# Row maxima in 64-row tiles and bf16, and another order on VectorE, in the output phase of an attention and recurrence kernel

## The chip, the cores and the metric

The kernel runs on one core of a Trainium2 chip. The metric is the device time of one execution in microseconds (us). In the rows PE is TensorE (matmul), PEld its weight loads, DVE is VectorE, ACT is ScalarE, POOL is GpSimd and SP is SyncE, which here issues the DMA transfers. L2267 is line 2267 of the kernel before.

## The reference

The input is x of 16 images, 64 by 64 positions, 128 channels. A first layer normalises x in channel groups, runs a two-dimensional recurrence over rows and columns and adds its result to x. The second layer takes the 4096 positions of an image as tokens t:

```
t = t + attention(ln(t))
t = t + ffn(ln(t))

attention: q, k, v = heads(ln(x) @ w_qkv), 8 heads of 16
           q_l, k_l = means of q and k over 64 landmarks
           attn1 = softmax(q @ k_l.T)        # 4096 x 64 for each head
           out = attn1 @ pinv(softmax(q_l @ k_l.T)) @ (softmax(q_l @ k.T) @ v)
           out = (out + conv33(v)) @ w_out + b_out
           return x + out
ffn:       Wx = x @ W.T, normalised with the statistics of all tokens,
           y_t = sigmoid(Wx_t + y_(t-1) @ V.T) along the tokens
```

The change touches attn1, the product with it, and the addition of the convolution.

## The kernel before

The program has phases one after the other: group norm, the recurrence over rows and columns, landmarks, pseudo-inverse (which also sets up constants for the next phase, class `Early`), output, and the final recurrence. The change lies in the output phase, and for one small constant at the end of the pseudo-inverse phase.

The output phase goes through the 16 images in 8 chunks of 512 tokens (NG = 8, GT = 4 tiles of 128 tokens). Every engine has its own program, a loop of 128 slots written out by hand; in each slot an engine works at several chunks at once, at different stages (`slot(b, c, ...)` handles chunk c + 1 for the row maxima, c for the scores and exponentials, c - 1 for reciprocals and merge, c - 2 for normalise and the addition of the convolution, c - 3 for the projection, c - 4 and c - 5 for the ffn). Engines run their instructions in order and meet only through semaphores; `wait(eng, name, count)` waits until `name` was raised count times. `nth(b, c)` is the running number of a chunk, from 1.

The stages of a chunk, with the engine and the line in the profile:

- GpSimd copies the queries to bf16, o_q_lp (L1931). kb_lp holds the keys of the landmarks in bf16 with the channels of other heads zeroed: 128 channels by 8 heads by 64 landmarks.
- TensorE, `row_maxima` (L2008): for each of the 4 token tiles one matmul of 128 channels, 128 tokens and 512 columns (8 heads of 64 landmarks), into the banks bank_l[0] and bank_l[1] in turn. Pairs of tiles are issued at two places in the slot.
- VectorE, `maxima` (L2230): a maximum over the 64 landmarks of each head, into o_m1 (in the rows o_m), 128 tokens by 128 places, of which two in each 16 are used.
- TensorE, `turn_maxima` (L2014): four transposes of o_m1 into bank_l[0]; ScalarE, `negate` (L2145), copies them with the opposite sign to o_negm in bf16.
- TensorE, `scores`: a matmul with o_negm (L2025) and then one with the queries (L2029) into the four banks bank_s; ScalarE takes exponentials (L2188) into o_p.
- TensorE, `weigh` (L2039): eight tiles of 64 rows and 32 columns side by side give the weighed values and the denominators; ScalarE copies them to `even` and `odd` (L2166, L2168).
- GpSimd masks `even` into o_pvs (L1937). SyncE packs the denominators by DMA, VectorE takes their reciprocals (L2273), SyncE spreads them to memory and broadcasts them back as o_rden.
- VectorE, `merge` (L2278): att = odd x keep + pvs. `normalise` (L2284): att = att x rden.
- The convolution of v: TensorE `convolve` (L2051), ScalarE `copy_convolved` (L2150) into o_res, TensorE `turn_convolved` (L2060) into bank_y. VectorE `add_convolved` (L2267): oT = att + bank_y.
- TensorE `project` (L2067) into bank_x; VectorE `residual` (L2243, then bn_stats and bn_aggr, L2249, into o_mv); GpSimd `norm`: o_vare (L1944), o_z (L1946), o_r (L1949), o_z again (L1951).
- TensorE `turn_normed` (L2074), ScalarE L2173, TensorE `ffn` (L2080), which writes bank_y and so waits until add_convolved has read it; ScalarE `copy_wx` (L2182); VectorE `statistics` (L2254, once per image also L2259).

TensorE's order in a slot is: scores, row maxima (two tiles), ffn, project, row maxima (two tiles), weigh, queries (L1999), turn_maxima, convolve, turn_convolved, turn_normed. VectorE's order is: four maxima, residual, reciprocals, merge, normalise, statistics, add_convolved. Once per image GpSimd also sets the next image's kb_lp (L1911), pairs and contexts (slots 2 to 5).

The functions that the diff touches:

Of the kernel before, what the change touches and what calls it, by code (L numbers as in the profile page):

```python
# [6 lines left out]
BF16 = mybir.dt.bfloat16  # L7
# [4 lines left out]
P = 128  # L12
# [1326 lines left out]
class Early:  # L1339


    def __init__(self, m, sems):
        self.w = m.sb("o_wq", [C, C])
        self.wo = m.sb("o_wo", [C, C])
        self.fw = m.sb("o_fw", [C, C])
        self.bout = m.sb("o_bout", [P, C])
        self.bands = m.sb("o_bands", [P, HEADS, LM])
        self.v = [[m.sb(f"o_v{k}{f}", [P, NT // 2, VROW]) for f in range(2)] for k in range(2)]
        self.xnT = [m.sb(f"o_xnT{k}", [C, 512]) for k in range(4)]
        self.bs = [m.sb(f"o_base{k}", [P, GT, C]) for k in range(4)]  # L1350
        self.pair_mask = m.sb("o_pair_mask", [C, 2, LM])
        self.kb_lp = [m.sb(f"o_kb_lp{k}", [C, HEADS, LM], BF16) for k in range(2)]
        self.zb = [m.sb(f"o_zb{k}", [P, PAIRS_H, 2 * DH]) for k in range(2)]
        self.keep = [m.sb(f"o_keep{h}", [P, 1]) for h in range(2)]
        self.ind = m.sb("o_ind", [P, 2, LM], BF16)
        self.m1 = m.sb("o_m1", [P, GT, P])
        self.half = m.sb("o_half", [P, GT])
        self.eps = m.sb("o_eps", [P, GT])
        self.one = m.sb("o_one", [P, 1])
        self.s = {n: sems.sem("o_" + n) for n in ("w", "const", "mask", "pair", "keep", "setup")}  # L1360
        self.s_band = sems.sem("o_band")
        self.s_v = [sems.sem(f"o_v{k}") for k in range(2)]
        self.s_xl = [sems.sem(f"o_xl{k}") for k in range(4)]
        self.s_bl = [sems.sem(f"o_bl{k}") for k in range(4)]
# [15 lines left out]
def pinv_phase(nc, sems, R, E, band, xnt, tokens, vals, taps, wqkv, w_out, b_out, ffn_wT):  # L1380
# [7 lines left out]
    with ExitStack() as ctx:  # L1388
# [267 lines left out]
        def _(dve):  # L1656
# [36 lines left out]
            for k in range(PINV_ITERS):  # L1693
# [7 lines left out]
                for c in LATE:  # L1701
                    if k + 1 < PINV_ITERS:
                        first_product(nc.vector, k + 1, c - 2, 0, s_ta)
                    last_product(k, c)
            nc.vector.tensor_reduce(E.pair_mask[:, :, :], R.head_mask[:, :, :].rearrange("c (g a) l -> c a l g", a=2), AX.X, ALU.add
                                    ).then_inc(E.s["pair"], 1)
            for h in range(2):
                taken = R.ident[:, DH * (1 - h):P:QUAD]
                nc.vector.tensor_reduce(E.keep[h][:, :], taken, AX.X, ALU.add).then_inc(E.s["keep"], 1)
                dve.wait_ge(E.s["keep"], 2 * h + 1)  # L1710
                nc.vector.tensor_scalar(E.keep[h][:, :], E.keep[h][:, :], -1.0, 1.0, ALU.mult, ALU.add).then_inc(E.s["keep"], 1)
# [6 lines left out]
def output_phase(nc, sems, R, E, xnt, tokens, vals, recips, t2, wx, wx_stats):  # L1718


    with ExitStack() as ctx:
# [268 lines left out]
        def _(pe):  # L1990
            pe.wait_ge(s["w"], 64)
            pe.wait_ge(s["const"], CONST)
            pe.wait_ge(s["mask"], PAIRS_H)

            def queries(b, c):

# [1 line left out]
                wait(pe, "qc", nth(b, c) - 1)  # L1998
                nc.tensor.matmul(bank_q[:, :], w[:, :], xnT[c % 4][:, :], start=True, stop=True).then_inc(s["qm"], 1)  # L1999

            def row_maxima(b, c, k, q):

                if k == 0:
                    wait(pe, "ql", nth(b, c))
                    wait(pe, "setup", SETUP * (b + (c == NG) + 1))
                    wait(pe, "neg", nth(b, c) - 1)
                wait(pe, "max", GT * (nth(b, c) - 1) + k - 1)
                nc.tensor.matmul(bank_l[k % 2][:, :], q_lp[c % 2][:, P * k:P * k + P],  # L2008
                                 kb_lp[q][:, :, :].rearrange("c h l -> c (h l)"), start=True, stop=True).then_inc(s["lp"], 1)

            def turn_maxima(b, c):
                wait(pe, "max", GT * nth(b, c))
                for k in range(GT):
                    mt = nc.tensor.transpose(bank_l[0][:, P * k:P * k + P], m1[:, k, :], R.ident[:, :])  # L2014
                mt.then_inc(s["mt"], 1)

            def scores(b, c, q):
# [64 lines left out]
            def slot(b, c, q, first, last):  # L2082
                scores(b, c, q)
                nq = q if c + 1 < NG else 1 - q
                if follows(c, 1, last):
                    row_maxima(b, c + 1, 0, nq)
                    row_maxima(b, c + 1, 1, nq)
                if precedes(c, 5, first):
                    ffn(b, c - 5)
                if precedes(c, 3, first):  # L2090
                    project(b, c - 3)
                if follows(c, 1, last):
                    row_maxima(b, c + 1, 2, nq)
                    row_maxima(b, c + 1, 3, nq)
                weigh(b, c, q)
                if follows(c, 3, last):
                    queries(b, c + 3)
# [11 lines left out]
            for c in range(NG):  # L2109
                wait(pe, "convc", c - 2)  # L2110
                convolve(0, c, bank_s[c % 3][:, :])
                if c in (1, 3):
                    queries(0, (c + 1) // 2)
                if c >= GT:
                    row_maxima(0, 0, c - GT, 0)
            turn_maxima(0, 0)
            wait(pe, "convc", NG)
            each_image(pe, slot)
# [103 lines left out]
        def _(dve):  # L2222
# [1 line left out]

            dve.wait_ge(s["keep"], 4)

            def maxima(b, c, k):
                wait(dve, "lp", GT * (nth(b, c) - 1) + k + 1)
                wait(dve, "mt", nth(b, c) - 1)
                nc.vector.tensor_reduce(m1[:, k, :].rearrange("p (g r) -> p g r", r=QUAD)[:, :, 0:2],  # L2230
                                        bank_l[k % 2][:, :].rearrange("p (g a l) -> p g a l", g=PAIRS_H, a=2), AX.X, ALU.max
                                        ).then_inc(s["max"], 1)

            def residual(b, c):
# [51 lines left out]
            def slot(b, c, q, first, last):  # L2286
# [4 lines left out]
                    residual(b, c - 3)  # L2291
                if precedes(c, 1, first):
                    reciprocals(b, c - 1)
                    merge(b, c - 1)
                if precedes(c, 2, first):
                    normalise(b, c - 2)
                if precedes(c, 5, first):
                    if c == 5 and b:
                        wait(dve, "stats", b)
                    statistics(b, c - 5)  # L2300
                if precedes(c, 2, first):
                    add_convolved(b, c - 2)
            for k in range(GT):
                maxima(0, 0, k)
            each_image(dve, slot)
# [310 lines left out]
```

## Time and profile before

| | |
|---|---|
| median of 3 runs | 6138.11 us (6130.87 to 6140.42) |
| profiled execution | 6141.54 us, span 6139.9 us |
| busy share of the span | PE 88%, ACT 52%, DVE 48%, POOL 30% |
| mean granted TensorE clock | 0.973 |
| output phase | first to last L2025 start, 2676.8 to 3776.0 us |

Busy shares of the whole span are means over phases with different limits; the final recurrence alone, after about 3830 us, leaves VectorE and GpSimd nearly idle. The rows further down are therefore taken from the output phase. A timeline row gives the start in us, the duration in us, engine, line, operation and operands, the count of instructions merged into the row, and in brackets the idle time of the engine before it and what ended it. The durations of TensorE's rows include a latency that overlaps the next group, so distances between starts are the better measure there.

### The profile page before, as it was taken

To read this page: it belongs to the slowest core of one execution; us is meant where nothing else is said; L and a number is where in the kernel's file an instruction comes from. 1 tells how busy PE (TensorE), PEld (TensorE's weight loads), DVE (VectorE), ACT (ScalarE), POOL (GpSimd) and SP (SyncE) were. 2 spreads that over 40 slices of the span, in tenths; PEclk is the share of its full clock that TensorE was granted. 3 is DMA by queue.
4 is the path that set the end of the run, shared out by engine and by line. 5 is a ranking of instruction groups with operands and counts; after the bars stand their busy time and mean duration, and the time that the engine had idled before them with its cause. 6 is when DMAs were issued, how large, how long until landed. Compare 5 with 4: busy or idle time off the path is not lost. (4 is left out here: it accounts for less than half of the span.)

```text
span 6139.9 us, 218886 instructions
## 1 busy us (share of the span) xinstructions
PE 5411.7 (88%) x89728; PEld 3294.7 (54%) x89728; DVE 2953.7 (48%) x7658; ACT 3195.0 (52%) x9222; POOL 1817.5 (30%) x2146
## 2 busy tenths in 40 slices
PE   5599999997899998789999997888888888888888
PEld 4499888996566665654555443333333333333333
DVE  8577666774777775458888886000000000000000
ACT  5455555564666665358888885333333333333333
POOL 2000000002877774248888886000000000000000
PEclk7799999998999999999999998999999999999999
DMA  8731111225777773347777775011111211111111
GB/s 352 282 108 60 56 56 63 76 84 179 238 232 230 217 230 103 94 127 219 220 219 223 217 219 151 26 44 46 44 46 44 60 45 46 44 46 44 46 46 44
DMA packets 857415, 756.44 MB, mean 123 GB/s; under 512 B 71024, under 2 KB 732528, under 8 KB 853360
## 3 DMA queue, kind: packets, MB, share of 16 engines
q1 hardware_dynamic: 840784, 640.78, 35.0%
q0 software_dynamic: 14208, 101.45, 4.1%
q8 instruction: 711, 11.65, 0.8%
q14 instruction: 272, 2.23, 0.1%
q10 hardware_dynamic: 1440, 0.33, 0.0%
HBM read 425.72 MB, written 308.45 MB: 120 GB/s over the span
## 5 line engine op out<-in xcount | busy, mean ns | idle before, releaser
L2554 ACT ACTIVATE f_y<-f_acc 128x16 f32<-128x16 f32 x4096 | 753.7, 184 | 1548.1 <-PE f_acc L2523 1548.1
L2523 PEld LDWEIGHTS f_acc<-f_y,f_vT 128*32 128x32 f32 x32768 | 647.0, 108 | 1493.0 <-ACT f_y L2554 1482.2
L2523 PE MATMUL f_acc<-f_y,f_vT 128*32 128x16 f32 x32768 | 1048.1, 193 | 297.9 <-issue 9.5
L2512 PE MATMUL f_junk<-f_idle 128*32 128x512 bf16 x12368 | 1228.4, 377 | 2.0 <-issue 1.9
L2470 DVE TENSOR_TENSOR f_sum<-f_turned,f_t 128x512 f32<-128x512 f32 x128 | 88.6, 692 | 1758.6 <-PE f_turned L2505 1758.5
L2230 DVE TENSOR_REDUCE o_m<-o_bank_l 128x8 f32<-128x512 f32 x512 | 329.4, 685 | 183.7 <-PE o_bank_l L2008 182.3
L533 POOL DMA_DIRECT2D hidden<-l_h x48 | 36.2, 756 | 1200.0 <-DVE l_hsum L733 973.3
L2512 PEld LDWEIGHTS f_junk<-f_idle 128*32 128x32 bf16 x12368 | 368.9, 99 | 2.2 <-issue 2.2
L1170 ACT ACTIVATE a_p<-a_s 128x512 f32<-128x512 f32 x512 | 264.2, 602 | 149.6 <-PE a_s L1055 149.6
L656 ACT ACTIVATE l_gate<-l_pf,l_bf 128x256 f32<-128x256 f32 (+7 forms) x512 | 202.3, 446 | 240.2 <-PE l_pf L583 215.8
L2188 ACT ACTIVATE o_p<-o_bank_s 128x512 f32<-128x512 f32 x512 | 264.4, 602 | 84.8 <-PE o_bank_s L2029 84.8
L2460 DVE TENSOR_SCALAR f_wxn<-f_wx,f_scale,f_shift 128x2048 f32<-128x2048 f32 x32 | 83.9, 2623 | 383.4 <-DMA f_wx<-wx 343.7
L573 PE MATMUL l_pf<-l_x,l_wf 128*128 128x256 f32 (+7 forms) x1024 | 240.2, 357 | 6.6 <-ACT l_gate L656 6.6
L1230 DVE TENSOR_REDUCE a_m3p<-a_s 128x1 f32<-128x512 f32 x384 | 235.6, 676 | 17.9 <-PE a_s L1031 17.9
L2505 PE MATMUL f_turned<-f_ident,f_y 128*32 128x128 f32 x4096 | 224.4, 292 | 1.0 <-issue 0.8
L2494 PE MATMUL f_acc<-f_wxn,f_ident 128*32 128x128 f32 x4096 | 210.2, 278 | 13.0 <-DVE f_wxn L2460 13.0
L941 POOL TENSOR_TENSOR a_r<-a_vare,a_half 128x8 f32<-128x8 f32 x128 | 209.6, 1638 | 10.0
L2158 ACT ACTIVATE o_base<-o_base,r_loss,r_gain 128x128 f32<-128x128 f32 x512 | 211.9, 506 | 0.0
L573 PEld LDWEIGHTS l_pf<-l_x,l_wf 128*128 128x128 f32 x1024 | 185.0, 191 | 23.6 <-ACT l_gate L656 7.8
L659 ACT ACTIVATE l_tanhc<-l_cell 128x256 f32<-128x256 f32 (+7 forms) x256 | 101.0, 395 | 177.8 <-DVE l_cell L709 177.8
L1946 POOL TENSOR_TENSOR o_z<-o_t,o_mv 128x512 f32<-128x512 f32 x128 | 186.4, 1457 | 0.0
L2080 PE MATMUL o_bank_y<-o_zT,o_fw 128*128 128x512 f32 x256 | 138.3, 622 | 35.9 <-DVE o_oT L2267 34.5
(280 smaller groups left out, 11906.8 us busy)
## 6 DMA issues: line engine op xcount, KB each, us to landing
o_v<-vals SPq DMA_DIRECT2D x256, 272.0 KB, 3.4
a_hid<-hidden SPq DMA_DIRECT2D x112, 520.0 KB, 4.7
hidden<-l_h POOLq DMA_DIRECT2D x48, 1040.0 KB, 6.2
skew<-gn_skew POOLq DMA_DIRECT2D x8, 6144.0 KB, 23.2
l_x<-skew SPq DMA_DIRECT2D x46, 1024.0 KB, 5.2
vals<-a_v SPq DMA_DIRECT2D x128, 272.0 KB, 3.5
gn_x<-in_x SPq DMA_DIRECT2D x16, 2048.0 KB, 15.5
a_xin<-in_x SPq DMA_DIRECT2D x128, 256.0 KB, 4.5
```

The lines of the kernel that those rows point to most:

```text
L573: mm = nc.tensor.matmul(banks[c][g][:, :, rows], w[W[g]][:, :], xs, start=g in (0, 2, 3), stop=False, skip_group_check=True)
L941: pool.tensor_tensor(r[:, :, :], vare[:, :, :], half[:, :, :], ALU.pow).then_inc(s["pow"], 1)
L1170: nc.scalar.activation(p3[c % 2][g][:, :], S[g][:, :], ACT.Exp).then_inc(s["exp"], 1)
L1230: nc.vector.tensor_reduce(m3p[:, g, c:c + 1], bank[:, :], AX.X, ALU.max).then_inc(s["mx"], 1)
L2158: nc.scalar.activation(bs[c % 4][:, k, :], bs[c % 4][:, k, :], ACT.Identity, scale=R.gain[:, b, n:n + 1], bias=R.loss[:, b, n:n + 1]).then ...
L2188: nc.scalar.activation(p1[g][:, :], bank_s[g][:, :], ACT.Exp).then_inc(s["exp"], 1)
L2230: nc.vector.tensor_reduce(m1[:, k, :].rearrange("p (g r) -> p g r", r=QUAD)[:, :, 0:2], bank_l[k % 2][:, :].rearrange("p (g a l) -> p g a ...
L2494: mm = nc.tensor.matmul(acc[k % 2][rows, PT * piece:PT * piece + PT, :], ident[:, rows], wxn[q][:, at, :], start=piece == 0, stop=False, s ...
L2505: mt = nc.tensor.matmul(turned[g % 2][rows, b % 4, :], y[q][:, rows, b], ident[:, :], start=True, stop=True)
L2512: nc.tensor.matmul(junk[rows, :], idle[:, 0:QUAD], idle[:, :], start=True, stop=True)
L2523: mm = nc.tensor.matmul(acc[k % 2][rows, t, :], vT[:, rows], before, start=False, stop=True, skip_group_check=True)
L2554: nc.scalar.activation(y[q][:, u, :], acc[u // RC % 2][:, u % RC, :], ACT.Sigmoid).then_inc(s_y, 1)
```

## The change

Row maxima: each token tile's matmul is split in two by channels, 64 rows with the four heads that have their channels there. The lower half of the channels writes bank_l[0], the upper half bank_l[1], and each bank now holds four heads of two token tiles. VectorE's maxima run over such a bank. o_m1 is bf16, and is turned by a matmul with a bf16 identity in place of an f32 transpose; the identity is cast once at the end of the phase before. On VectorE normalise and add_convolved come before merge and statistics.

```diff
-        self.m1 = m.sb("o_m1", [P, GT, P])
+        self.m1 = m.sb("o_m1", [P, GT, P], BF16)
+        self.ident_lp = m.sb("o_ident_lp", [P, P], BF16)
...
+            nc.vector.tensor_copy(E.ident_lp[:, :], R.ident[:, :]).then_inc(E.s["pair"], 1)
...
+            pe.wait_ge(s["pair"], 2)
...
-            def row_maxima(b, c, k, q):
+            def row_maxima(b, c, r, q):
-                if k == 0:
+                if r == 0:
                     wait(pe, "ql", nth(b, c))
                     wait(pe, "setup", SETUP * (b + (c == NG) + 1))
                     wait(pe, "neg", nth(b, c) - 1)
-                wait(pe, "max", GT * (nth(b, c) - 1) + k - 1)
-                nc.tensor.matmul(bank_l[k % 2][:, :], q_lp[c % 2][:, P * k:P * k + P],
-                                 kb_lp[q][:, :, :].rearrange("c h l -> c (h l)"), start=True, stop=True).then_inc(s["lp"], 1)
+                for k in range(2):
+                    for half in range(2):
+                        if k == 0:
+                            wait(pe, "max", GT * (nth(b, c) - 1) + 2 * r + half - 1)
+                        rows, heads = slice(LM * half, LM * half + LM), slice(PAIRS_H * half, PAIRS_H * half + PAIRS_H)
+                        token = P * (2 * r + k)
+                        ml = nc.tensor.matmul(bank_l[half][:, 2 * P * k:2 * P * k + 2 * P], q_lp[c % 2][rows, token:token + P],
+                                              kb_lp[q][rows, heads, :].rearrange("c h l -> c (h l)"), start=True, stop=True)
+                        if k == 1:
+                            ml.then_inc(s["lp"], 1)
...
-                    mt = nc.tensor.transpose(bank_l[0][:, P * k:P * k + P], m1[:, k, :], R.ident[:, :])
+                    mt = nc.tensor.matmul(bank_l[0][:, P * k:P * k + P], m1[:, k, :], E.ident_lp[:, :], start=True, stop=True)
...
                 if follows(c, 1, last):
                     row_maxima(b, c + 1, 0, nq)
-                    row_maxima(b, c + 1, 1, nq)
...
                 if follows(c, 1, last):
-                    row_maxima(b, c + 1, 2, nq)
-                    row_maxima(b, c + 1, 3, nq)
+                    row_maxima(b, c + 1, 1, nq)
...
-            def maxima(b, c, k):
-                wait(dve, "lp", GT * (nth(b, c) - 1) + k + 1)
+            def maxima(b, c, n):
+                r, half = n // 2, n % 2
+                wait(dve, "lp", GT * (nth(b, c) - 1) + n + 1)
                 wait(dve, "mt", nth(b, c) - 1)
-                nc.vector.tensor_reduce(m1[:, k, :].rearrange("p (g r) -> p g r", r=QUAD)[:, :, 0:2],
-                                        bank_l[k % 2][:, :].rearrange("p (g a l) -> p g a l", g=PAIRS_H, a=2), AX.X, ALU.max
+                nc.vector.tensor_reduce(m1[:, 2 * r:2 * r + 2, LM * half:LM * half + LM].rearrange("p k (g r) -> p k g r", r=QUAD)[:, :, :, 0:2],
+                                        bank_l[half][:, :].rearrange("p (k g a l) -> p k g a l", k=2, g=2, a=2), AX.X, ALU.max
...
                     reciprocals(b, c - 1)
-                    merge(b, c - 1)
                 if precedes(c, 2, first):
                     normalise(b, c - 2)
+                    add_convolved(b, c - 2)
+                if precedes(c, 1, first):
+                    merge(b, c - 1)
                 if precedes(c, 5, first):
                     if c == 5 and b:
                         wait(dve, "stats", b)
                     statistics(b, c - 5)
-                if precedes(c, 2, first):
-                    add_convolved(b, c - 2)
```

Ahead of the first image the row maxima are issued in two groups in place of four.

## Rows read from the trace of the kernel before

**Rows 1.** The tile o_negm: count, duration ns min/median/max, first and last start us.
```profile
L2025 PE MATMUL o_bank_s<-o_negm,o_ind x512: 371/384/385, 2676.8 to 3776.0; 32*128 32x512 bf16 x171
```

**Rows 2.** Busy us of each engine in one stretch, granted clock, DMA share, GB/s.
```profile
3000.00:3100.00 100.00, 99.17 (x755) 50.77 (x740) 83.68 (x215) 83.65 (x175) 89.71 (x88) 1.00 0.77 222
```

**Rows 3.** Timeline of TensorE, one slot.
```profile
3021.09 0.39 PE L2025 MATMUL o_bank_s<-o_negm,o_ind 32*128 32x512 bf16 x4
3021.32 1.02 PE L2029 MATMUL o_bank_s<-o_qT,o_kb 32*128 32x512 f32 x8
3022.28 0.61 PE L2008 MATMUL o_bank_l<-o_kb_lp,o_q_lp 128*128 128x512 bf16 x2
3022.72 1.02 PE L2080 MATMUL o_bank_y<-o_zT,o_fw 128*128 128x512 f32 x2
3023.58 1.05 PE L2067 MATMUL o_bank_x<-o_wo,o_oT 128*128 128x128 f32 x8
3024.47 0.59 PE L2008 MATMUL o_bank_l<-o_kb_lp,o_q_lp 128*128 128x512 bf16 x2
3024.99 1.09 PE L2039 MATMUL o_bank_s<-o_p,o_zb 64*32 64x512 f32 x16
3026.01 1.12 PE L1999 MATMUL o_bank_s<-o_xnT,o_wq 128*128 128x512 f32 x2
3026.97 0.60 PE L2014 MATMUL o_bank_l<-r_ident,o_m 128*128 128x128 f32 x4
3027.50 1.11 PE L2051 MATMUL o_bank_s<-o_v,o_bands 128*64 128x256 f32 x8
3028.54 0.66 PE L2060 MATMUL o_bank_y<-r_ident,o_res 128*128 128x128 f32 x4
...
3029.57 0.39 PE L2025 MATMUL o_bank_s<-o_negm,o_ind 32*128 32x512 bf16 x4
```

**Rows 4.** Timeline of VectorE, the same slot.
```profile
3022.70 1.29 DVE L2230 TENSOR_REDUCE o_m<-o_bank_l 128x8 f32<-128x512 f32 x2 [0.47 <-PE o_bank_l L2008]
3024.88 1.29 DVE L2230 TENSOR_REDUCE o_m<-o_bank_l 128x8 f32<-128x512 f32 x2 [0.89 <-PE o_bank_l L2008]
...
3028.28 0.66 DVE L2278 SCALAR_TENSOR_TENSOR o_att<-o_odd,o_keep,o_pvs 128x512 f32<-128x512 f32 x1
3028.85 0.69 DVE L2284 TENSOR_TENSOR o_att<-o_att,o_rden 128x512 f32<-128x512 f32 x1
...
3030.06 0.67 DVE L2267 TENSOR_TENSOR o_oT<-o_att,o_bank_y 128x512 f32<-128x512 f32 x1
```

**Rows 5.** Timeline of ScalarE, the same slot.
```profile
3022.42 2.06 ACT L2188 ACTIVATE o_p<-o_bank_s 128x512 f32<-128x512 f32 x4 [0.63 <-PE o_bank_s L2029]
...
3028.66 0.60 ACT L2150 ACTIVATE o_res<-o_bank_s 128x512 f32<-128x512 f32 x1 [0.22 <-PE o_bank_s L2051]
```

**Rows 6.** Timeline of GpSimd, the same slot.
```profile
3028.21 0.79 POOL L1944 TENSOR_TENSOR o_vare<-o_mv,o_eps 128x4 f32<-128x4 f32 x1 [0.94 <-DVE o_mv L2249]
3028.95 1.49 POOL L1946 TENSOR_TENSOR o_z<-o_t,o_mv 128x512 f32<-128x512 f32 x1
3030.40 1.01 POOL L1949 TENSOR_TENSOR o_r<-o_vare,o_half 128x4 f32<-128x4 f32 x1
```

**Rows 7.** Timeline of all engines, the slot after kb_lp is set.
```profile
3050.69 1.28 POOL L1911 TENSOR_TENSOR o_kb_lp<-r_head_mask,r_k_lm 128x512 bf16<-128x512 f32 x1
...
3054.13 0.75 DVE L2278 SCALAR_TENSOR_TENSOR o_att<-o_odd,o_keep,o_pvs 128x512 f32<-128x512 f32 x1 [0.32 <-POOL o_pvs L1937]
3054.20 1.58 POOL L1946 TENSOR_TENSOR o_z<-o_t,o_mv 128x512 f32<-128x512 f32 x1
3054.80 1.53 DVE L2284 TENSOR_TENSOR o_att<-o_att,o_rden 128x512 f32<-128x512 f32 x1
3055.75 1.46 POOL L1949 TENSOR_TENSOR o_r<-o_vare,o_half 128x4 f32<-128x4 f32 x1
...
3057.67 1.10 PE L2080 MATMUL o_bank_y<-o_zT,o_fw 128*128 128x512 f32 x2 [0.83 <-DVE o_oT L2267]
```

More of the change, by code:

```diff
@@ L2113, in _ @@
                     queries(0, (c + 1) // 2)
-                if c >= GT:
-                    row_maxima(0, 0, c - GT, 0)
+                if c in (GT, GT + 2):
+                    row_maxima(0, 0, (c - GT) // 2, 0)
             turn_maxima(0, 0)
```

## The prediction

> **What bounds the kernel now.** I first looked up where the touched lines run. Everything in the diff, apart from one small cast, lies in the output phase: the first and last start of the bank_s matmuls fed by o_negm [rows 1] are 1099.2 us apart for 128 chunks, so 127 slots (a slot is the work of one 512-token chunk) take 8.655 us each. The share table of one stretch in the middle [rows 2] shows TensorE busy 99% at a granted clock of 1.00, GpSimd 90%, VectorE and ScalarE 84% each, and the DMA engines 77%. So TensorE comes first, but nobody is idle by more than a sixth: whatever TensorE gives up, another engine may take back.
>
> TensorE's timeline of one slot [rows 3] has no wait in it. From bank_s at 3021.09 to the next at 3029.57 is 8.48 us. I read it by distances between starts, since the rows' own durations include a latency that overlaps the next group. The first pair of row-maxima matmuls takes 0.44 (3022.28 to 3022.72), the second 0.52, the turn of the maxima 0.53. Two 512-column bf16 matmuls in 0.44 make 0.21 each, and eight 128-column f32 passes (L2067) in 0.89 make 0.11 each.
>
> VectorE in the same slot [rows 4] waits twice for row-maxima matmuls, 0.47 and 0.89 us, so it needs 8.48 - 1.36 = 7.1. ScalarE [rows 5] starts its exponentials at 3022.42 and ends the copy of the convolution, which the next scores need, at 3029.26. GpSimd [rows 6] waits 0.94 for VectorE's bn_aggr before o_vare.
>
> One slot per image is different [rows 7]. GpSimd first makes the next image's kb_lp (1.28 us), is late for o_pvs, VectorE's merge starts late, its normalise takes 1.53 us instead of 0.69, add_convolved is late, and the ffn matmul on TensorE, which overwrites the bank that add_convolved reads, waits 0.83. The mean slot of 8.655 against the regular 8.48 is this: 8 x 0.175 = 1.4 us per image, 22 us in 16 images.
>
> **The change, part by part, per slot.**
>
> *Row maxima in 64-row tiles.* Four matmuls of 128 rows by 512 columns become eight of 64 rows by 256 columns, in four pairs whose members use different rows and different banks. No 64-row bf16 pair is in the trace. The nearest row is L2029: eight f32 passes over 512 columns on four row groups take 0.96 us (3021.32 to 3022.28), where two such passes on all rows (L2080) take 0.86 [rows 3]. Four row groups thus run side by side, and so should two. Then four pairs of 256 columns stream 4 x 0.107 = 0.43 in place of 0.85: a saving of 0.43. Bounds: 0 if pairs do not overlap, 0.43 if they do.
>
> *Changes of tile shape.* Where the shape of the tile stays, groups follow each other at the streaming time: L2008 to L2080 0.44 for 0.43 streamed, L2080 to L2067 0.86. Where it changes, about 0.1 is added: L2029 (32 rows) to L2008 (128) 0.96 instead of 0.86, L2008 to L2039 (64 by 32) 0.52 instead of 0.43, L2039 to L1999 1.02 instead of 0.86 [rows 3]. The new row maxima put a 64 by 128 shape ahead of the ffn matmul and after project, where there was no change before. Two more changes at 0.1 cost 0.2. Bounds 0 and 0.3 (two of L2039's 0.16). I take 0.2. The Trainium skill (TensorEngine Tiling, Key Properties) says that changing the tiling mode drains TensorE, which speaks against this part of the change; it has no price, the rows agree with it, and without it the sum would be 0.2 per slot lower.
>
> *The turn in bf16.* Four f32 passes in 0.53, of which about 0.1 is the change to the 128 by 64 shape behind it. bf16 halves the streaming: the bf16 matmul took 0.21 for 512 columns, so four of 128 stream 0.21 instead of 0.43. Weight loads may keep it from showing; L1999 to L2014 has another 0.1 that may go with the transposing form. Bounds 0 and 0.3; I take 0.2.
>
> TensorE's slot without waits is then 8.48 - 0.43 + 0.2 - 0.2 = 8.05 (bounds 7.75 and 8.58).
>
> *ScalarE.* From the first exponential to the end of the convolution's copy 6.84, of which 0.22 is a wait; then bank_s, scores and the next exponential, 1.33 after the matmul starts [rows 3, 5]: 6.62 + 0.06 + 1.33 = 8.01, a little under 8.05. No charge.
>
> *VectorE, the maxima.* The same 512 elements from one bank and eight results; writing bf16 costs and saves nothing that I can see in a reduce bound by its input. 0. The first result comes after the third of four small matmuls, about when the first big one ended: 0.
>
> *VectorE, the order.* After the reciprocal came merge, normalise, statistics, add; now normalise, add, merge, statistics. The work is the same, so the gain is only that add is earlier by a merge and a statistics (0.6 + 0.6). That removes the 0.83 wait of the ffn matmul [rows 7]. What comes with it: add now directly follows normalise, whose result it needs, a start distance of about 0.72 instead of 0.60; and add needs the turned convolution (L2060), which ends at 3029.20; the instruction after the reciprocal starts at 3028.28 [rows 3, 4]. Measured from the second pair of row maxima (3024.47) that end is 4.73, less 0.2 and 0.1 of the savings behind it 4.43; add is ready 3.81 + 0.72 = 4.53 after it. Hidden, by 0.1.
>
> *VectorE against GpSimd.* In regular slots o_vare and o_z are stretched while merge and normalise run: z takes 1.49 [rows 6], and ends 0.9 after normalise does. In the late slot z took 1.58, and then normalise took 1.53: it had to wait for z, ending 0.55 after z did; add and the maxima, with one operand in PSUM, are never stretched [rows 4, 7]. So the two engines exclude each other when VectorE reads two operands from SBUF. The Trainium skill (SBUF — State Buffer, Who interferes with whom) states just this, that whoever starts first holds the port for its whole instruction; these rows agree. In the new order (n is the start of normalise) o_vare is blocked until n + 0.68, z starts at n + 0.7 and nothing blocks it during add, so it runs to n + 1.74. Merge is ready at n + 1.3 and is blocked until then: it ends at n + 2.3 instead of n + 1.85, 0.45 later. Bounds 0 and 0.85 (the stretched normalise). I take 0.45.
>
> Does VectorE still fit? Its loop is: the second row maxima start on TensorE, 0.41 until the reduce starts (3024.47 to 3024.88), 5.18 to add's start, 0.6 to its end, then two more maxima, 1.29, and 0.06 until TensorE may overwrite the second bank [rows 3, 4]. That is 7.54, plus 0.45 blocked = 7.99. Under 8.05, by very little.
>
> *GpSimd.* z gets 0.45 shorter (1.49 to 1.04), r 0.45 longer as it now runs into the blocked merge (1.01 and 1.46 in [rows 6, 7]). Zero in sum. Its wait of 0.94 shrinks by the slot's 0.43 to 0.51.
>
> *Once per image.* kb_lp takes GpSimd 1.28 [rows 7], with the step to the next instruction about 1.35; 0.51 is cover, so about 0.85 reaches normalise (now the first to meet a late GpSimd), less 0.06 of VectorE's slack: 0.8. wx_stats is written by one more VectorE instruction, about 0.2. Together 1.0 per image instead of 1.4, 0.12 per slot.
>
> *Other parts.* The cast of the identity in the phase before, and a wait for it, fall where VectorE has nothing else due: under 0.3 us once. No DMA is moved; SyncE's spread still follows the reciprocal, which keeps its place, and the DMA share rises to 0.77 x 8.48 / 8.17 = 0.80.
>
> **The sum.** Regular slot 8.05, mean 8.17. 127 x (8.655 - 8.17) = 62 us. The profiled execution took 6141.5 us (span 6139.9), so 6080; the median of the runs, 6138.1, lies 3.4 below it, so 6077.
>
> **The rivals.**
> - *The pairs do not overlap* (or weight loads, twice as many, fill the time). TensorE 8.48 + 0.2 - 0.2 = 8.48; only the ffn wait goes, say 17 us: 6121. Against it: L2029.
> - *Nothing takes back the gain*: no price on tile changes, merge not blocked or absorbed. 7.85, mean 7.96, 88 us: 6050. For it: VectorE's 7.54 would allow it. Against: 0.1 shows at each shape change, and ScalarE's 8.01 would have to give.
> - *Slower*: GpSimd stays late in every slot, so that normalise waits for the rest of o_pvs as well as merge for z. At the 0.85 of the late slot VectorE's loop is 7.99 + 0.85 = 8.84, 127 x 0.185 = 24 us more: 6162. It decides once GpSimd's cover of 0.51 is gone in regular slots and normalise loses over 0.67 in each. Against it: a longer slot gives GpSimd its cover back, so the state should heal itself.
> - *VectorE sets the pace*, with TensorE near 7.9: mean 8.15, 6075, the same number by another road.
>
> **Chances and range.** My forecast (TensorE or VectorE at 8.0 to 8.15, so 6062 to 6095) 0.52; pairs or tile changes eating most of the gain (6095 to 6125) 0.20; the whole gain (6040 to 6062) 0.15; no change 0.04; slower 0.09. A measurement of this kernel tells about 0.2% (12 us) from no change. The range 6045 to 6115 leaves out the slower case, no change, and the ends of the two beside. Faster by over 0.2%: 0.87; within: 0.04; slower: 0.09.
>
> **What would show it.** Starts of the row-maxima groups: first to ffn about 0.33, second to weigh about 0.33, with project to row maxima 0.95. The turn to the convolution about 0.33. No wait of the ffn matmul for o_oT. Merge (L2278's line) near 1.1 us, o_r near 1.46, o_z near 1.04. VectorE's wait ahead of the first maxima nearly gone. I am wrong if the four small matmuls of a group take 0.43 or more, or if normalise is stretched in regular slots, or if TensorE waits for o_m in every slot.

## The result, and the profile after

The changed kernel takes 6087.5 us (median of 4 runs, 6082.1 to 6091.8) against 6138.7 for the kernel before: ratio 0.9918, 95% interval 0.9904 to 0.9932, so 0.8% or 51 us faster. The forecast was 6077 in a range of 6045 to 6115.

The gain lies in the output phase. The tile o_negm in the trace of the changed kernel (count, duration ns min/median/max, first and last start us):

```profile
L2035 PE MATMUL o_bank_s<-o_negm,o_ind x512: 371/384/385, 2674.2 to 3726.8; 32*128 32x512 bf16 x171
```

1052.6 us for 127 slots, 8.288 each, where [rows 1] gave 8.655: 46.6 of the 51.3 us between the two profiled executions (6141.5 and 6090.2). The other 4.7 us lie before the first slot and after the last. The share table of the stretch of [rows 2] (us, PE, PEld, DVE, ACT, POOL, clock, DMA share, GB/s):

```profile
3000.00:3100.00 100.00, 98.64 (x822) 49.67 (x816) 88.11 (x218) 85.97 (x181) 90.58 (x90) 1.00 0.80 229
```

TensorE is still full, VectorE went from 84 to 88%, the DMA engines from 77 to 80%. One regular slot on TensorE, beside [rows 3]:

```profile
3003.76 0.39 PE L2035 MATMUL o_bank_s<-o_negm,o_ind 32*128 32x512 bf16 x4
3003.99 1.02 PE L2039 MATMUL o_bank_s<-o_qT,o_kb 32*128 32x512 f32 x8
3004.95 0.39 PE L2016 MATMUL o_bank_l<-o_kb_lp,o_q_lp 64*128 64x256 bf16 x4
3005.27 1.12 PE L2090 MATMUL o_bank_y<-o_zT,o_fw 128*128 128x512 f32 x2
3006.23 1.05 PE L2077 MATMUL o_bank_x<-o_wo,o_oT 128*128 128x128 f32 x8
3007.22 0.39 PE L2016 MATMUL o_bank_l<-o_kb_lp,o_q_lp 64*128 64x256 bf16 x4
3007.54 1.09 PE L2049 MATMUL o_bank_s<-o_p,o_zb 64*32 64x512 f32 x16
3008.56 1.12 PE L2002 MATMUL o_bank_s<-o_xnT,o_wq 128*128 128x512 f32 x2
3009.52 0.39 PE L2024 MATMUL o_bank_l<-o_ident_lp,o_m 128*128 128x128 bf16 x4
3009.84 1.11 PE L2061 MATMUL o_bank_s<-o_v,o_bands 128*64 128x256 f32 x8
...
3011.90 0.40 PE L2035 MATMUL o_bank_s<-o_negm,o_ind 32*128 32x512 bf16 x4
```

The slot is 8.14 instead of 8.48. Group by group, from one group's start to the next one's: first row maxima to ffn 0.32 (was 0.44), second to weigh 0.32 (0.52), the turn 0.32 (0.53). Those are savings of 0.12, 0.20 and 0.21. But two distances grew: ffn to project 0.96 (0.86) and project to row maxima 0.99 (0.89).

VectorE and GpSimd around the same place, beside [rows 4] and [rows 6]:

```profile
3011.05 0.63 DVE L2293 TENSOR_TENSOR o_att<-o_att,o_rden 128x512 f32<-128x512 f32 x1
3011.71 0.69 DVE L2276 TENSOR_TENSOR o_oT<-o_att,o_bank_y 128x512 f32<-128x512 f32 x1
3012.31 0.96 DVE L2287 SCALAR_TENSOR_TENSOR o_att<-o_odd,o_keep,o_pvs 128x512 f32<-128x512 f32 x1
3013.19 0.68 DVE L2263 BATCH_NORM_STATS2 o_fst<-o_wx 128x6 f32<-128x512 f32 x1
3013.80 1.26 DVE L2239 TENSOR_REDUCE o_m<-o_bank_l 128x8 bf16<-128x512 f32 x2
```

```profile
3010.97 0.75 POOL L1946 TENSOR_TENSOR o_vare<-o_mv,o_eps 128x4 f32<-128x4 f32 x1 [0.75 <-DVE o_mv L2258]
3011.69 1.03 POOL L1948 TENSOR_TENSOR o_z<-o_t,o_mv 128x512 f32<-128x512 f32 x1
3012.69 1.46 POOL L1951 TENSOR_TENSOR o_r<-o_vare,o_half 128x4 f32<-128x4 f32 x1
```

Merge runs 0.96 instead of 0.65, until 0.55 after the end of o_z; o_z is 1.03, o_r 1.46; the wait ahead of the first maxima is gone. That is the picture that the prediction drew for a regular slot. What it did not draw is in the table of waits from 2750 to 3700 us (us in total, times, longest):

```profile
PEld o_bank_l L2016 <- DVE o_m L2239: 14.8, 43, 0.5
DVE o_rec_packed L2282 <- DMA o_den_packed<-o_odd: 13.5, 28, 1.2
PE o_bank_l L2016 <- DVE o_m L2239: 5.9, 30, 0.3
PE o_bank_y L2090 <- DVE o_oT L2276: 1.6, 4, 0.8
```

The same table of the kernel before has these lines for the ffn matmul and the reciprocal:

```profile
PE o_bank_y L2080 <- DVE o_oT L2267: 18.5, 27, 0.9
DVE o_rec_packed L2273 <- DMA o_den_packed<-o_odd: 1.6, 4, 0.6
```

The ffn matmul hardly waits any more, but the reciprocal now waits for the packed denominators in 28 slots instead of 4. Distances between slot starts on TensorE split into three kinds: 8.14 to 8.17 in most, 8.4 to 8.6 in most slots after kb_lp, and 27 slots of 8.6 to 9.4. The kernel before had 8.47 to 8.51 in most, one of about 9.55 in 13 of the images (mostly with one of 8.6 behind it), and fourteen more of 9.1 to 9.6.

How a late transfer makes such a slot is seen where the slot that starts at 2869.88 takes 8.70. VectorE, GpSimd and TensorE around it:

```profile
2869.09 0.35 DVE L2282 RECIPROCAL o_rec_packed<-o_den_packed 128x32 f32<-128x32 f32 x1 [0.24 <-DMA o_den_packed<-o_odd]
2869.36 1.32 DVE L2293 TENSOR_TENSOR o_att<-o_att,o_rden 128x512 f32<-128x512 f32 x1
...
2872.58 1.27 DVE L2239 TENSOR_REDUCE o_m<-o_bank_l 128x8 bf16<-128x512 f32 x2
```

```profile
2868.93 0.20 POOL L1946 TENSOR_TENSOR o_vare<-o_mv,o_eps 128x4 f32<-128x4 f32 x1 [0.63 <-DVE o_mv L2258]
2869.08 1.04 POOL L1948 TENSOR_TENSOR o_z<-o_t,o_mv 128x512 f32<-128x512 f32 x1
```

```profile
2873.91 0.39 PE L2016 MATMUL o_bank_l<-o_kb_lp,o_q_lp 64*128 64x256 bf16 x3 [0.17 <-DVE o_m L2239]
```

The reciprocal waits only 0.24, but that makes normalise start 0.28 after o_z instead of ahead of it. Normalise then ends 0.56 after o_z does and takes 1.32 instead of 0.63; the maxima are late, TensorE waits for them in the second group of row maxima, and the slot is 0.56 longer than a regular one. All 27 late slots have such a start: in 21 of them the normalise around the slot's start took over 0.9 (in 14 of these 21 the reciprocal ahead of it had waited for the denominators), and in the other 6 that wait alone was 0.67 or more.

### The profile page after: what moved, and what is told of

Read it like the earlier page. It is cut to its first block and busy times, and to the rows that moved or that the text cites. A ratio compares the mean times of both kernels' runs of the same rounds, so it can differ in the third digit from the quotient of the medians.

```text
span 6088.6 us, 219912 instructions
## 1 busy us (share of the span) xinstructions
PE 5375.2 (88%) x90240; PEld 3269.6 (54%) x90240; DVE 2974.9 (49%) x7659; ACT 3178.0 (52%) x9222; POOL 1809.8 (30%) x2146
## 5 line engine op out<-in xcount | busy, mean ns | idle before, releaser
L2239 DVE TENSOR_REDUCE o_m<-o_bank_l 128x8 bf16<-128x512 f32 x512 | 327.2, 680 | 100.0 <-PE o_bank_l L2016 100.0
L1951 POOL TENSOR_TENSOR o_r<-o_vare,o_half 128x4 f32<-128x4 f32 x128 | 185.7, 1451 | 0.0
L2077 PEld LDWEIGHTS o_bank_x<-o_wo,o_oT 128*128 128x128 f32 x1024 | 136.8, 195 | 61.8 <-issue 61.8
```

Source lines behind the costliest of these rows:

```text
L2239: nc.vector.tensor_reduce(m1[:, 2 * r:2 * r + 2, LM * half:LM * half + LM].rearrange("p k (g r) -> p k g r", r=QUAD)[:, :, :, 0:2], bank_l ...
```

## The experiments

Every ratio is to the kernel before on the same chip. The changed kernel has 0.9918.

**The changed kernel with VectorE's old order.**

```diff
                     reciprocals(b, c - 1)
+                    merge(b, c - 1)
                 if precedes(c, 2, first):
                     normalise(b, c - 2)
-                    add_convolved(b, c - 2)
-                if precedes(c, 1, first):
-                    merge(b, c - 1)
...
                     statistics(b, c - 5)
+                if precedes(c, 2, first):
+                    add_convolved(b, c - 2)
```

> The changed kernel with VectorE's old order (merge, normalise, statistics, add). Theory: TensorE's regular slot stays 8.14 us in streaming, but the addition of the convolution now ends 0.1 to 0.2 us after the ffn matmul could start, so regular slots come to 8.2 to 8.3 and the slot after kb_lp loses over 1 us again; mean slot 8.40, 14 us slower than the changed kernel (about 6102). Rival, that the order brought nothing and TensorE's shorter work everything: within 5 us of the changed kernel (6087). Rival, that the order brought most: 6120 or more.

Measured: 0.9998 (0.9989 to 1.0007). The gain is gone, all of it. Of the times expected only the last, 6120 or more, came true, though the theory's regular slot of 8.2 to 8.3 was nearly met. Its waits and slots say why. TensorE (waits from 2750 to 3700 us):

```profile
PE o_bank_y L2090 <- DVE o_oT L2276: 49.1, 71, 2.8
```

Regular slots are 8.30 to 8.37, not 8.14, since the addition ends too late for the ffn matmul; the slots after kb_lp are about 9.8 in nine images; some twenty others take 9.2 to 9.4, and one 12.6. Two neighbouring slots of it, a regular one and a late one, VectorE, GpSimd and TensorE:

```profile
2740.11 0.65 DVE L2287 SCALAR_TENSOR_TENSOR o_att<-o_odd,o_keep,o_pvs 128x512 f32<-128x512 f32 x1
...
2748.60 1.51 DVE L2287 SCALAR_TENSOR_TENSOR o_att<-o_odd,o_keep,o_pvs 128x512 f32<-128x512 f32 x1
```

```profile
2740.03 0.79 POOL L1946 TENSOR_TENSOR o_vare<-o_mv,o_eps 128x4 f32<-128x4 f32 x1 [0.79 <-DVE o_mv L2258]
2740.78 1.49 POOL L1948 TENSOR_TENSOR o_z<-o_t,o_mv 128x512 f32<-128x512 f32 x1
...
2748.37 0.20 POOL L1946 TENSOR_TENSOR o_vare<-o_mv,o_eps 128x4 f32<-128x4 f32 x1 [0.78 <-DVE o_mv L2258]
2748.52 1.04 POOL L1948 TENSOR_TENSOR o_z<-o_t,o_mv 128x512 f32<-128x512 f32 x1
```

```profile
2752.05 1.10 PE L2090 MATMUL o_bank_y<-o_zT,o_fw 128*128 128x512 f32 x2 [1.17 <-DVE o_oT L2276]
```

In the first slot merge starts 0.08 after o_vare and both of GpSimd's instructions stretch. In the second merge starts 0.23 after it; o_vare and o_z are served first, merge takes 1.51, and the ffn matmul waits 1.17. A tenth or two on VectorE decides which engine pays, and in the old order the addition stands behind both of VectorE's two-operand instructions and passes all of it to TensorE.

**The new order alone, in the kernel before.** The last part of the diff and nothing else.

> The kernel before with only VectorE's new order. Theory: TensorE's 8.48 us per slot stays and binds, only the waits of the ffn matmul go: mean slot 8.52 instead of 8.655, 17 us faster than before (6121). Rival, that the blocked merge costs VectorE as much as the earlier addition gains: 6138 or slower. Merge about 1.0 us instead of 0.65 and o_z 1.04 instead of 1.49 in regular slots under both.

Measured: 0.9950 (0.9936 to 0.9963), 31 us. The direction is right, the size nearly twice what I gave it. o_z is 1.04 in most slots as expected, but merge is 0.7 to 0.8 and not 1.0. Slots are 8.47 to 8.54, and one of about 8.7 per image; both the 9.55 and the fourteen others are gone.

**The turn in bf16 alone, in the kernel before.**

```diff
-        self.m1 = m.sb("o_m1", [P, GT, P])
+        self.m1 = m.sb("o_m1", [P, GT, P], BF16)
...
-                    mt = nc.tensor.transpose(bank_l[0][:, P * k:P * k + P], m1[:, k, :], R.ident[:, :])
+                    mt = nc.tensor.matmul(bank_l[0][:, P * k:P * k + P], m1[:, k, :], E.ident_lp[:, :], start=True, stop=True)
```

> The kernel before with only o_m1 in bf16 and its turn by a bf16 matmul. Theory: the turn takes 0.32 instead of 0.53 between starts, nothing else on TensorE moves: regular slot 8.27 us, once-per-image loss as before or 0.3 more, mean 8.45 to 8.49, 21 to 26 us faster (6112 to 6117). Rival, that a matmul with the identity costs as much as the transpose and the gain in the changed kernel came from the tiles: 6138.

Measured: 0.9984 (0.9975 to 0.9993), 10 us, and so neither the 21 to 26 of the theory nor the nothing of the rival. Regular slots came down to 8.26 to 8.29 as expected, 27 us over 127 slots, but late slots (about 9.75 after kb_lp, others 9.1 to 9.3) took two thirds of it back.

**The changed kernel without 64-row tiles.**

```diff
-                for k in range(2):
-                    for half in range(2):
...
+                nc.tensor.matmul(bank_l[k % 2][:, :], q_lp[c % 2][:, P * k:P * k + P],
+                                 kb_lp[q][:, :, :].rearrange("c h l -> c (h l)"), start=True, stop=True).then_inc(s["lp"], 1)
```

> The changed kernel with the row maxima in 128-row tiles again (bf16 turn and new order stay). Theory: the tiles gave 0.12 us per regular slot and no more (they save 0.12 and 0.20 at their own groups and cost 0.10 each on ffn's and project's way to the next group), so the regular slot is 8.27 and the kernel 12 to 15 us slower than the changed one (about 6100). Rival, that the four pairs saved their full 0.43 and another engine took 0.3 back: TensorE's regular slot above 8.4 and 6110 or more. Rival, that VectorE or the DMAs set the pace anyway: the same 6087.

Measured: 0.9930 (0.9916 to 0.9943), 43 us faster than before and so about 8 slower than the changed kernel; the two intervals overlap. The slot decides between the theories: 8.26 to 8.29 where the changed kernel has 8.14 to 8.17. In this kernel ffn to project is 0.86 again:

```profile
3007.39 1.02 PE L2083 MATMUL o_bank_y<-o_zT,o_fw 128*128 128x512 f32 x2
3008.25 1.05 PE L2070 MATMUL o_bank_x<-o_wo,o_oT 128*128 128x128 f32 x8
3009.14 0.59 PE L2011 MATMUL o_bank_l<-o_kb_lp,o_q_lp 128*128 128x512 bf16 x2
```

So the tiles are worth 0.12 us per slot: they save 0.12 and 0.20 at their own groups and add 0.10 on each side of project. No other engine took 0.3 back.

**Only the second group in 64-row tiles.** The first group is one matmul of 128 rows by 512 columns for each token tile again, and its maxima likewise.

```diff
+                if r == 0:
+                    for k in range(2):
...
+                        nc.tensor.matmul(bank_l[k][:, :], q_lp[c % 2][:, token:token + P],
+                                         kb_lp[q][:, :, :].rearrange("c h l -> c (h l)"), start=True, stop=True).then_inc(s["lp"], 1)
+                    return
```

> The changed kernel with 64-row tiles only for the second group of row maxima (between project and weigh); the first group, between the scores and the ffn matmul, is 128 rows by 512 columns again. Theory from the distances between starts: the first group saves 0.12 at its own place and costs 0.10 on the ffn matmul's way to the next group, so undoing it costs 0.02 us per slot: slots of 8.16, the same time as the changed kernel within 4 us (-0.75 to -0.82%). Rival, that each group of tiles is worth the same: slots of 8.20, 8 us slower than the changed kernel (-0.69%).

Measured: 0.9934 (0.9920 to 0.9948). The slots are 8.15 to 8.19, about 0.02 above the changed kernel's, as the distances said: nearly all that the tiles bring is brought by the second group. The total can't tell the two expectations apart.

**Statistics ahead of merge.**

```diff
                     add_convolved(b, c - 2)
-                if precedes(c, 1, first):
-                    merge(b, c - 1)
...
                     statistics(b, c - 5)
+                if precedes(c, 1, first):
+                    merge(b, c - 1)
```

> The changed kernel with VectorE's order normalise, add, statistics, merge. Merge then starts when o_z on GpSimd is over, so it is not blocked (0.65 instead of 0.89 mean), and VectorE's loop is about 0.4 us shorter. Theory, that in regular slots TensorE sets the pace and the rest comes from late packed denominators: regular slots stay 8.14, the late ones shrink a little because VectorE catches up sooner; 0 to 0.1% faster than the changed kernel (-0.82 to -0.92% against before). Rival, that the blocked merge is what makes late slots: 0.2% or more faster than the changed one.

Measured: 0.9958 (0.9944 to 0.9971), slower than the changed kernel by 0.4%; both expectations failed. Most slots are still 8.14 to 8.16, but thirty take 9.2 or more. In one of them normalise ran 1.32 and merge 1.30, each behind an instruction of GpSimd, and TensorE waited for maxima:

```profile
3017.31 1.32 DVE L2293 TENSOR_TENSOR o_att<-o_att,o_rden 128x512 f32<-128x512 f32 x1
...
3019.88 1.30 DVE L2287 SCALAR_TENSOR_TENSOR o_att<-o_odd,o_keep,o_pvs 128x512 f32<-128x512 f32 x1
...
3021.10 1.27 DVE L2239 TENSOR_REDUCE o_m<-o_bank_l 128x8 bf16<-128x512 f32 x2
```

```profile
3019.59 1.04 POOL L1953 TENSOR_TENSOR o_z<-o_z,o_r 128x512 f32<-128x512 f32 x1
3020.59 1.72 POOL L1961 TENSOR_TENSOR o_base<-o_base,o_bout 128x512 f32<-128x512 f32 x1
```

Merge started 0.3 after GpSimd's second o_z and had to wait for its end. In a regular slot merge is now free, 0.65, as expected. But once normalise has been late, merge meets a second instruction of GpSimd: the late slot costs 1.1 instead of 0.6, and there are thirty of them. In the changed kernel a regular merge meets only the last 0.4 us of the first o_z, which costs no time.

**Packing the denominators early,** in the changed kernel and, as a control, in the kernel before.

```diff
                     spread(b, c - 1)
+                pack(b, c)
...
                     broadcast(b, c - 1)
-                pack(b, c)
```

> The changed kernel with one move on SyncE: the packing of the denominators is issued right behind the spread of the reciprocals, ahead of the loads of v and of the broadcast. Theory, that the slots of 8.7 us and more in the changed kernel come from a reciprocal that waits for the packed denominators (28 waits): these waits vanish, slots stay at 8.14 but for the ones after kb_lp, the mean falls from 8.29 to about 8.18, and the kernel is 0.20 to 0.25% faster than the changed one (-1.05% against before). Rival, that the late slots come from the lock between VectorE and GpSimd: the waits vanish and the time stays at -0.82%. Rival, that the DMA queues are full: the broadcast or the loads of v come late instead, and the time stays or grows.

> The kernel before with the packing of the denominators issued early, as the only edit. Theory: at 8.48 us per slot the denominators are late in 4 slots of 128, so the edit is worth nothing before the change: within 0.1% of before. Rival, that SyncE's order cost something all along: 0.2% or more faster than before.

Measured: 1.0061 (1.0047 to 1.0074) in the changed kernel, 1.0051 (1.0037 to 1.0064) in the kernel before. The third way given for the changed kernel came true; for the control neither expectation did. Waits for packed denominators are gone, and normalise waits for the broadcast instead, first in the changed kernel and then in the kernel before:

```profile
DVE o_att L2293 <- DMA o_rden<-recips: 90.6, 96, 2.4
DVE o_att L2284 <- DMA o_rden<-recips: 26.8, 41, 2.5
```

Lateness moved from one transfer to the other and grew.

**A lighter load of v,** in the changed kernel and in the kernel before.

```diff
+            lanes = slice(0, 1 if light and side else P)
-            sp.dma_start(self.v[half][side][:, GT * piece:GT * piece + GT, :],
-                         vals[b, row:row + 512, :].rearrange("(n p) c -> p n c", p=P)).then_inc(self.s_v[half], 16)
+            sp.dma_start(self.v[half][side][lanes, GT * piece:GT * piece + GT, :],
+                         vals[b, row:row + 512, :].rearrange("(n p) c -> p n c", p=P)[lanes]).then_inc(self.s_v[half], 16)
```

> The changed kernel with a lighter load of v: in the output phase one of the two shifted copies of v is loaded for one partition only (the convolution of the later images is then computed from old data for that copy; every instruction of the engines stays, and so does the number of transfers). Theory, that the changed kernel's slots of 8.7 us and more come from transfers that land late because the DMA engines are at 80%: the waits for the packed denominators go from 28 to under 5, the mean slot falls from 8.29 to about 8.18, 13 to 16 us faster than the changed kernel (about -1.05% against before). Rival, that they come from the lock between VectorE and GpSimd: -0.82% as the changed kernel, within 0.05%.

> The control of the run with the lighter load of v: the same edit in the kernel before (same part of the convolution computed from old data). Theory, that at 8.48 us per slot transfers are in time and the late slots are those of the lock: within 0.15% of before, with slots of 9.2 and 9.55 us still there. Rival, that the DMA engines cost the kernel before just as much: 0.25% or more faster than before.

Measured: 0.9920 (0.9907 to 0.9933) and 0.9998 (0.9989 to 1.0007). The share table of the first, from 2750 to 3700 us:

```profile
2750.00:3700.00 950.00, 941.14 (x7763) 472.36 (x7762) 850.31 (x2073) 820.91 (x1717) 875.96 (x858) 1.00 0.69 195
```

and its wait for the denominators:

```profile
DVE o_rec_packed L2283 <- DMA o_den_packed<-o_odd: 11.8, 22, 1.6
```

The DMA engines went from 80 to 69% busy, and the denominators are late almost as often, 22 times instead of 28. The slots stay as well: 24 of 8.6 and more, against 27. My theory that the load of the DMA engines makes them late fails at this step of load, and the time is that of the rival. In the kernel before the theory was right: no effect on the median that can be measured, and late slots still there. In the profiled execution 5 of the 14 others remain; whether that is the edit or chance is open, as only one execution was traced.

**The loads of v behind the packing.**

```diff
                     spread(b, c - 1)
+                    broadcast(b, c - 1)
+                pack(b, c)
...
-                if precedes(c, 1, first):
-                    broadcast(b, c - 1)
-                pack(b, c)
```

> The changed kernel with SyncE's loads of v behind the broadcast and the packing, so that the small transfers of the reciprocals no longer share the DMA engines with them. Theory, that late small transfers are what makes slots late: the wait of the broadcast for the spread shrinks from 0.8 us, packed denominators land earlier, the mean slot falls by 0.05 to 0.1, 6 to 12 us faster than the changed kernel (-0.95%). Rival, as in the run that packed early, that the loads of v now pile up on the broadcast and make it late: slower than the changed kernel by 10 us or more.

Measured: 1.0276 (1.0258 to 1.0293). Slower, though not by the rival's road: the convolution on TensorE waits for v in every fourth slot, which takes 15 to 18 us. The denominators are not earlier either; the reciprocal waits for them 42 times, 63.3 us.

```profile
PE o_bank_s L2060 <- DMA o_v<-vals: 135.5, 24, 7.0
```

```profile
2750.00:3700.00 950.00, 806.05 (x6258) 406.39 (x6260) 684.29 (x1669) 662.05 (x1383) 692.24 (x694) 0.92 0.63 187
```

**GpSimd relieved.**

```diff
-                pool.tensor_tensor(tile, tile, bout[:, :].unsqueeze(1).broadcast_to([P, GT, C]), ALU.add).then_inc(s["based"], 1)
+                pool.tensor_tensor(tile[:, 0:1, :], tile[:, 0:1, :], bout[:, :].unsqueeze(1), ALU.add).then_inc(s["based"], 1)
```

> The changed kernel with GpSimd's addition of the output bias done for one token tile of four (three quarters of the tokens lack the bias), which frees GpSimd by about 0.9 us in each slot. Theory, that a late GpSimd costs the changed kernel 0.3 us in the slot after kb_lp and little else: 4 to 6 us faster than the changed kernel (-0.9% against before), and slots of 8.7 us still there. Rival, the sum of the prediction, in which kb_lp costs 0.8 us per image: 12 us or more faster (-1.02%).

Measured: 0.9932 (0.9920 to 0.9943), not faster than the changed kernel, so that both expected times were missed. The slots after kb_lp came down to 8.14 in seven of the images, where the changed kernel has that in three; that is the 0.3 us that the theory gave them, but there are 40 slots of 8.6 and more instead of 27, with 33 waits for denominators, 20.4 us. Why a freer GpSimd brings more of these waits was not looked into. The prediction's 0.8 us per image for a late GpSimd does not show, here or in the slots of the changed kernel.

## Why the prediction was right, and where its sum was off

The forecast of 62 us met 51, and the sign, the engine that sets the pace and the shape of a regular slot were right. Yet its terms were wrong by more than the sum shows, and that they met is partly luck. In the sum TensorE's shorter slot (8.48 to 8.05) made 55 us and the order 7. Measured one after the other, the order made 31, the turn on top of it about 12 and the tiles about 8. (The sum's upper bound for TensorE's slot should also have been 8.78, not 8.58: 8.48 + 0.3 with nothing saved.)

- **Row maxima in tiles: too large.** The pairs do overlap: a group takes 0.32, as forecast. The step that failed is "Two more changes at 0.1 cost 0.2". I had one cost at the end of the first group, inside its 0.33, and one behind project. Both came, and a third with them, 0.10 between ffn and project, where the shape does not change. Net 0.12 us per slot instead of 0.23 (the untiled run: 8.27 against 8.14), 15 us of streaming in place of 29. [rows 3] had a row for it. L1999, which also follows narrow tiles, takes 0.96 to the next group instead of 0.86, and I had put that down to the transposing turn behind it. In the traces it is the first matmul behind the change that is longer: 0.53 to the next matmul's start, in L1999 of both kernels and in the ffn of the changed one, against 0.43 in the ffn of regular slots before and in the untiled run. The Trainium skill (TensorEngine Tiling (Array Packing), Key Properties) says that changing the tiling mode drains TensorE. The costs here agree with it, as those on both sides of project are gone without the tiles; it gives no price.
- **The turn: right for the regular slot,** 0.21 against 0.20, which is 27 us over 127 slots. Under the new order only about 12 of them reached the time, and 10 under the old one; late slots took the rest. The other 0.1, from L1999 to the turn, stayed with the transposing form gone: 0.96 in both kernels.
- **The new order: too small.** The sum gave it 7 us (1.0 us per image instead of 1.4), a rival the 0.83 wait in one slot per image, 17 us; alone it gave 31. The step that failed is "The mean slot of 8.655 against the regular 8.48 is this", which reads one kind of late slot only. That mean hides that the last image's slots are shorter, and that fourteen more slots were late. In 7 of these fourteen merge took over 1.2, in 5 others normalise: they lost the race against o_z. I had shown the lock in both directions but only priced it in the new order.
- **The parts are not a sum.** With the old order, 0.33 less in TensorE's slot brings nothing (0.9998). Order alone 31 us, tiles and turn alone 1 us, together 51. The order is what lets TensorE's saving through. In [rows 3, 4] the addition ends at 3030.73 and the next ffn matmul is due at 3022.72 + 8.48 = 3031.20, so it was 0.47 ahead; the savings that lie between the second row maxima and the ffn matmul are 0.20 + 0.21 + 0.12 = 0.53. With the old order the addition is late in every slot; the regular ones lose 0.17 us to it and the others more. I had credited TensorE's saving to TensorE alone.
- **VectorE against GpSimd: right in kind.** Merge blocked by o_z, o_z free, o_r blocked, in the rows as drawn; 0.31 instead of 0.45 in the slot shown, and hidden in regular slots. What I had named as a sign of being wrong, normalise stretched, does not happen in regular slots, but it does ahead of most late ones: it took over 0.9 us 29 times in 128. So the lock did not go with the new order; it moved from merge to normalise. The Trainium skill (SBUF — State Buffer, Who interferes with whom) says that issue order decides who waits. The two slots of the old-order run agree in the main: merge, 0.23 behind o_vare, found o_z at work and waited. But with 0.08 between the starts it was the earlier one, o_vare, that waited (0.79 instead of 0.20), so starts that lie within a tenth do not tell who comes first.
- **DMA: the missing term.** "No DMA is moved" was no argument. The loop from reciprocal over spread, broadcast and pack to the next reciprocal was never priced, and a shorter slot ran into it: 28 waits, 13.5 us, in place of 4 and 1.6. 20 of the 27 slots of 8.6 and more begin with one. The trace shows the way from the wait to the late slot (2869.09 and behind): normalise starts a few tenths late and meets o_z. That this is what holds the kernel at 8.29 instead of 8.17 is still argued from the slots; no run took the waits away and left the rest alone, since packing early made the broadcast late instead. Why the denominators are late was not settled. It is not a load of 80% instead of 69%. The transfers' latency and SyncE's order of issue are left, and so is why the early pack delays the broadcast so much.
- **Once per image:** about 0.3 us after kb_lp, not 0.8.

No version here beats the changed kernel. Of those that keep all of the work, five more are faster than the kernel before (the order alone, the turn alone, untiled, second group, statistics first); only the intervals of the untiled and second-group ones overlap with its own.

## What to carry to other kernels

When the engine that sets the pace gets less work, look up by how much each of its partners was ahead of it; an addition that was 0.47 us ahead of the ffn matmul was late once 0.53 had been saved in between, and the edit that moves such a partner is worth more than its own waits in the profile show. Before calling a regular slot the rule, list the lengths of all slots: 27 late ones held 25 us in the kernel before, and the new order removed all but 3.5 of them. Where two engines lock each other out, look at what shifts their starts: a wait of 0.24 us made a slot 0.56 longer. And price every loop through a DMA, also the ones where no transfer is moved.

## What the runs showed of the hardware

- Two engines that exclude each other make a race. In the two slots of the old-order run merge took 0.65 us when it started 0.08 us after GpSimd's o_vare, and 1.51 us when it started 0.23 us after it. In that run, apart from its first slots, every merge of over 1.2 us started 0.18 to 0.46 us after the nearest o_vare, and every one that started 0.07 to 0.16 us after it took 0.75 us or less.
- A change of tile shape costs about 0.10 us on TensorE in the group ahead of it (project to row maxima 0.99 with, 0.89 without), and in two f32 groups of 128 rows behind it another 0.10 in their first matmul (ffn to project 0.96 with, 0.86 without).
- Taking the DMA engines from 80 to 69% busy left the lateness of small transfers nearly as it was (22 waits in about 115 slots, from 28).
- With TensorE waiting for v up to 7.0 us at a time (24 times, 135.5 us), its granted clock was 0.92 on average from 2750 to 3700 us, where the other kernels had 1.00. After one such wait, of 6.01 us, it was 0.50 for the next 2 us, the lower of its two levels, and the convolution's eight matmuls took 1.98 us instead of 1.1.
